# Eight experts on sorted rows: both expert layers in two halves and blocks of 256 rows, and the fourth level in two lanes

## The reference

```python
x = x + tanh(g_xattn[0]) * L0_xattn(ctx, layernorm(x))      # "a0": 16 heads, keys from the context
x = x + tanh(g_ffn[0])   * L0_ffn(layernorm(x))             # 128 -> 512 -> 512 -> 512 -> 128, dense
x = x + tanh(g_xattn[1]) * L1_xattn(layernorm(x), ctx)      # "a1": 16 heads, context and own keys
x = x + tanh(g_ffn[1])   * L1_ffn(layernorm(x))             # "af": causal attention, then 8 experts
x = x + tanh(g_xattn[2]) * L2_xattn(ctx, layernorm(x))      # "a2": 8 heads, keys from the context
x = x + tanh(g_ffn[2])   * L2_ffn(layernorm(x))             # 8 experts
x = x + tanh(g_xattn[3]) * L3_xattn(layernorm(x), ctx)      # per-token norm, W_in, plus a context part
x = x + tanh(g_ffn[3])   * L3_ffn(layernorm(x))             # quantized 128 -> 512 -> 128

# the experts of L1 (E = 8, two per token, F = 256); L2 is alike with F = 512, gelu and biases
probs = softmax(t @ router_w);  vals, idx = top_k(probs, 2);  w = vals / sum(vals)
gate = sum(one_hot(idx, 8) * w[..., None], axis=1)
hid = silu(einsum('td,edf->tef', t, w1)) * einsum('td,edf->tef', t, w3)
y = einsum('ted,te->td', einsum('tef,efd->ted', hid, w2), gate)
```

## Time and profile before

| | |
|---|---|
| median of 3 runs | 2380.14 us (2370.82 to 2387.39) |
| profiled execution, its own time | 2380.9 us |
| its span, first to last instruction | 2379.1 us |
| PE busy | 2093.7 us, 88% |
| DVE busy | 1531.5 us, 64% |
| ACT busy | 1066.7 us, 45% |
| POOL busy | 606.8 us, 26% |
| mean granted clock of TensorE | 0.902 |

### The profile page before, as it was taken

How to read it: one execution, slowest core, us unless ns; L and a number is a source line. 1 busy time by engine, 2 the same in 40 slices (tenths; PEclk the granted TensorE clock), 3 DMA queues, 4 the chain that set the end, 5 groups by cost and what they waited for, 6 DMA issues and landing times. The chain is left out here.

```text
span 2379.1 us, 40889 instructions
## 1 busy us (share of the span) xinstructions
PE 2093.7 (88%) x15206; PEld 1293.5 (54%) x15206; DVE 1531.5 (64%) x4178; ACT 1066.7 (45%) x1905; POOL 606.8 (26%) x867
## 2 busy tenths in 40 slices
PE   3688889998588888799999999988899999999993
PEld 1455556676476666455654556544554555555552
DVE  5677665432577776577747766557855677776655
ACT  2344533332355556244543434424354556555542
POOL 3421002001422221232202322243301233433232
PEclk9888889999789999799999999985569999999995
DMA  7556300300455554121200200016520000000001
GB/s 191 108 124 125 65 1 15 57 1 1 82 93 104 105 103 111 36 53 42 57 16 1 45 1 1 1 60 142 128 57 25 10 10 10 9 10 10 10 1 36
DMA packets 153138, 121.94 MB, mean 51 GB/s; under 512 B 21980, under 2 KB 145828, under 8 KB 147236
## 3 DMA queue, kind: packets, MB, share of 16 engines
q1 hardware_dynamic: 152940, 119.32, 23.0%
HBM read 78.04 MB, written 39.85 MB: 50 GB/s over the span
## 5 line engine op out<-in xcount | busy, mean ns | idle before, releaser
L1841 DVE TENSOR_REDUCE mneg<-psb 128x4 f32<-128x512 f32 (+1 forms) x576 | 388.7, 685 | 168.4 <-PE psb L1441 165.8
L2139 ACT ACTIVATE HB<-psb 128x512 f32<-128x512 f32 x384 | 226.7, 598 | 203.7 <-PE psb L1441 200.7
L1441 PE MATMUL psb<-K,Q 96*128 96x128 bf16 x1280 | 192.4, 256 | 54.7 <-DVE mneg L1841 32.7
L1440 PE MATMUL psb<-HB,KS 128*128 128x512 f32 x512 | 232.9, 598 | 0.0
L1441 PE MATMUL psb<-Q,K 99*128 99x128 bf16 x1280 | 150.3, 251 | 79.6 <-DMA Q<-mT 79.4
L1982 DVE TENSOR_TENSOR OE<-psb,OE 128x512 f32<-128x512 f32 x120 | 82.7, 689 | 191.1 <-ACT OE L2211 190.4
L2321 POOL TENSOR_SCALAR rs<-mv 128x2 f32<-128x2 f32 (+1 forms) x104 | 24.0, 230 | 712.0 <-DVE mv L1799 704.0
L2211 ACT ACTIVATE OE<-psb 128x512 f32<-128x512 f32 x128 | 76.5, 597 | 287.6 <-PE psb L1440 287.3
L2139 ACT ACTIVATE HB<-psb,bias 128x512 f32<-128x512 f32 x192 | 131.9, 687 | 145.4 <-PE psb L1441 143.8
L2207 ACT ACTIVATE HB<-psb,cols 128x512 f32<-128x512 f32 x256 | 171.3, 690 | 44.5 <-PE psb L1440 43.2
L1441 PEld LDWEIGHTS psb<-K,Q 96*128 96x128 bf16 x1280 | 112.1, 113 | 132.3 <-issue 61.5
(11 more groups left out here) (347 smaller groups left out, 4637.4 us busy)
## 6 DMA issues: line engine op xcount, KB each, us to landing
K<-sc_k SPq DMA_DIRECT2D x32, 384.0 KB, 5.0
Q<-sc_q SPq DMA_DIRECT2D x32, 384.0 KB
sc_q<-comp SPq DMA_DIRECT2D x48, 192.0 KB, 2.3
sc_q<-comp SPq DMA_DIRECT2D x48, 128.0 KB, 2.1
vraw<-in_ctx SPq DMA_DIRECT2D x48, 128.0 KB, 6.9
KS<-sc_s SPq DMA_DIRECT2D x16, 384.0 KB
K<-sc_k SPq DMA_DIRECT2D x32, 192.0 KB, 3.6
Q<-sc_q SPq DMA_DIRECT2D x32, 192.0 KB, 4.4
```

Source lines behind the costliest of these rows:

```text
L1440: return pe.e.matmul(out, w, x, start=start, stop=stop)
L1441: return pe.e.matmul(out, w, x, start=start, stop=stop, skip_group_check=True)
L1841: t = e.tensor_reduce(m.mneg[:, s.b % 4, s.i * A.per:(s.i + 1) * A.per], PSB[s.use.bank].rearrange("p (h k) -> p h k", h=A.per), AX.X, ALU ...
L2139: a.done(act(m.HB[:, s.slot, :], PSB[s.use.bank], ACT.Exp, bias=bz), s.use.drained)
```

## The change

Both expert layers leave the dense form. `sorted_front` replaces `front`: after the ranks it keeps the two chosen experts of each token (`gate_pick`), counts with small bf16 matmuls how many earlier tokens chose the same expert (`place`), and writes each token's normalized row twice to a DRAM array `tok_rows`, into the region of the chosen expert (`scatter`, eight indirect DMAs of 128 rows issued by POOL per group). When four groups (half of the tokens) are written, `blocks` computes on DVE a table of 24 blocks of 256 rows (16 full ones' worth plus 8, always 24, the spare ones on rows of zeros) and runs them as a pipeline: load, transpose, choice of the expert's weights through a value read from the table into a register (ACT copies them to a fixed place; PE, DVE and SP read table values too), up, activation, down, store to `y_rows`. `fetch` reads a sequence's two result rows per token back (two indirect DMAs on POOL), `combine` adds them with their gates (three DVE instructions of 128 elements).

Where the work lies: all 8 fronts of the first layer run beside af, its half 0 (24 blocks) beside the end of af, its half 1 beside the first nine steps of a2, together with fetches and combines for all 32 sequences; the 8 fronts of the second layer run beside a2. Its 48 blocks follow a2. The fourth level has two sets of buffers: even groups and odd groups are two chains; those of groups 0 to 3 are begun with half 1's blocks, those of groups 4 to 7 after the last block. Silu is made from tanh. The second norm's scale comes from the first's variance (`twice`), on POOL, which saves a pass on DVE. x is stored in eight DMAs, one per group. At the start of `ffn0` 17 DMAs issued by ACT fill `tok_rows` with zeros. The core of the diff:

```diff
+BLK = 256
+HALF = B * S // 2
+ROWS = HALF + BLK
+FULL = 2 * HALF // BLK
+NBLK = FULL + 8
+SPARE = 16 * ROWS
...
+        def n9():
+            do("scatter", g=g, i=E.i, xf=E.xf[k], need=(got["n"], got["p"], t_zero, E1.loaded[h] if E.i else None))
+            E.scattered[k] = dma(f"dma_scatter{k}", 8)
...
+        return [*([(n0, 4)] if E.i else []), (n1, 4), (n2, 7 if E.i == 0 else 4), (n3, 4), (n4, 4), n5, n6, n7, n8, n9]
+
+    def blocks(E, h, t_w, start, bank):
...
+        def first(n):
+            for j in ([0, 1] if n == 0 else [n + 1]):
+                if j < NBLK:
+                    do("block_load", i=E.i, h=h, j=j, need=(c.tab, E.sorted[h], start), free=t_full.get(j - 3))
+                    loaded[j] = dma(f"dma_xs{j % 3}")
+            if n < NBLK:
+                u = use(bank(), "act")
+                do("block_turn", i=E.i, h=h, j=n, use=u, need=(loaded[n], start), free=up_full.get(n - 2))
...
+                do("block_weights", i=E.i, h=h, j=n, need=(c.tab, t_w), free=up_full.get(n - 2), done=w_ready[n])
+        def second(n):
+            if 0 <= n - 1 < NBLK:
...
+                do("block_up", i=E.i, h=h, j=j, ua=ua, ub=ub, need=(turned[j], w_ready[j]), tanh=t, h_free=(down_full.get(j - 2), c.idx))
...
+            if 0 <= n - 2 < NBLK:
...
+                do("block_down", i=E.i, h=h, j=j, use=u, need=(h_done[j], t_w), free=stored.get(j - 3), bias=t_2.get("b2"))
+                do("block_store", i=E.i, h=h, j=j, need=u.drained)
...
+    AF.slots = 6
...
+    A2.side = 3
+    begin2, run2, *_ = attention(A2, prep_ctx(A2, "sc_q3", False), finish2, hold={8: 10, 9: 11})
...
+    fetch1(4)
...
+    chain(blocks(E1, 1, t_m, after_f1, misc), 1)
+    begin2()
+    chain([lambda n=n: fetch1(n) for n in range(5, 13)], 2)
+
+    def more(t):
+        if t == 9:
+            while E1.stored[1] is None:
+                slot_no[0] += 1
+                run_side(1)
+            do("moe2_load", need=E1.done[1])
+            t_2["w"] = dma("dma_moe2", 2)
+        fetch1(min(t + 13, 16) if t < 9 else max(t + 13, 19 + 3 * (t - 9)))
+
+    run2(more)
+    while side:
+        slot_no[0] += 1
+        run_side(1)
...
+    for i, unit in enumerate(blocks(E2, 0, t_2["w"], after_a2, bank)):
+        unit()
+        if i == 0:
+            chain([*setup, *[f for g in range(NG) for f in context(g)]], 2)
+        for _ in range(4):
+            tick()
+    for k in range(2):
+        chain([*results(k), *own(k), *results(k + 2), *own(k + 2)], 2)
+    for unit in blocks(E2, 1, t_2["w"], after_a2, bank):
+        unit()
+        for _ in range(4):
+            tick()
+    misc_turn[1] = 8
+    for k in range(2):
+        chain([*results(k + 4), *own(k + 4), *results(k + 6), *own(k + 6)], 2)
...
     def block_up(s):                                   # PE: weights 128x128, 256 columns, fp32
+        for u, at_ in ((s.ua, 0), (s.ub, 256)):
+            for c in range(2):
+                t = matmul(PSB[u.bank][:, 256 * c:256 * c + 256], w[:, at_ + 128 * c:at_ + 128 * c + 128], x, c == 0, c == 1, False)
     def block_down(s):                                 # PE: n = 256 or 512 hidden features
+        at_ = table(s.i, s.h, 2 if s.i == 0 else 1, s.j, 7 * n)
+        for i in range(2):
+            for c in range(n // 128):
+                t = matmul(o[:, 128 * i:128 * i + 128], h[:, 256 * c + 128 * i:256 * c + 128 * i + 128], w[:, bass.ds(at_ + 128 * c, 128)],
+                           i == 0 and c == 0, c == n // 128 - 1, False)
     def combine(s):                                    # DVE
+        for k in range(2):
+            v.wait_ge(v.step(e.scalar_tensor_tensor(out=u, in0=y[:, 128 * k:128 * k + 128], scalar=m.gk[:, s.i, k, s.b:s.b + 1], in1=u, op0=ALU.mult, op1=ALU.add)))
+        v.done(e.scalar_tensor_tensor(out=x, in0=u, scalar=tg[:, s.gi:s.gi + 1], in1=x, op0=ALU.mult, op1=ALU.add), s.done)
     def scatter(s):                                    # POOL
+        for j in range(4):
+            for k in range(2):
+                e.indirect_dma_start(m.tok_rows, bass.IndirectOffsetOnAxis(ap=m.pidx[:, s.i, k, 4 * s.g + j:4 * s.g + j + 1], axis=0), ...)
```

More of the change, by code:

```diff
@@ L484, in k_store, with attention @@
             k_load(p + 2)
-    def attention(A, prep, finish, may=lambda p, what: True):
+    def attention(A, prep, finish, may=lambda p, what: True, hold={}):
         H, n_s, n_st, lag = A.H, A.n_s, A.n_st, A.lag
@@ L617, in run @@
                 for pp in range(NP):
-                    if pp not in ahead and max(0, load_step[pp] - {2: 5, 4: 3 if A.causal else 2, 8: 2}[n_st]) == tstep:
+                    if pp not in ahead and max(hold.get(pp, 0), load_step[pp] - {2: 5, 4: 3 if A.causal else 2, 8: 2}[n_st]) == tstep:
                         coming[pp] = prep(pp)
@@ L1055, in make_plan, with end1 @@
     t_2 = {}
+    do("moe1_load", need=pe_after_ffn0)
+    t_m = dma("dma_moe1", 2)
+    E1.begin = now()
+    for q in range(4):
+        do("va_ones", q=q, need=va_free[q])
+        va_free[q] = inc("pool", "clear_pool")
+    def end1(h):
+        if h == 0:
+            chain(blocks(E1, 0, t_m, E1.begin, misc), 2)
+    E1.end = end1
+    run_f1()
+    while side:
+        slot_no[0] += 1
+        run_side(1)
+    after_f1 = now()
     def finish2(b, k, t):
         finish_add(2)(b, k, t)
-        if b in (3, 7):
-            front2(b // 4, ("AT", 0), "big_at")
@@ L1178, in make_plan, with fetch1 @@
-    do("moe2_wait", need=t_w2)
+        if b % 4 == 3:
+            chain(sorted_front(E2, b // 4), 2)
+    A2.side = 3
+    begin2, run2, *_ = attention(A2, prep_ctx(A2, "sc_q3", False), finish2, hold={8: 10, 9: 11})
+    E2.begin, E2.end = after_f1, lambda h: None
+    fetched = [0]
+    def fetch1(upto):
+        while fetched[0] < min(upto, B):
+            b = fetched[0]
+            combine(E1, b, fetch(E1, b, after_f1))
+            fetched[0] += 1
+    do("moe2_small_load")
+    t_2["bg"] = dma("dma_bg")
@@ L1375, in make_plan, with results, fetched @@
-    moe(6, up2, init2, each2, lambda g: chain(own3["own"](g), 1))
+    setup, context, own = layer3(after_a2)
+    ring[1], misc_turn[1] = 5, 3
+    def results(g):
+        got = {}
+        def fetched(b):
+            got[b] = fetch(E2, b, after_a2)
+        return [*[lambda b=b: fetched(b) for b in range(4 * g, 4 * g + 4)], *[lambda b=b: combine(E2, b, got[b]) for b in range(4 * g, 4 * g + 4)]]
+    for i, unit in enumerate(blocks(E2, 0, t_2["w"], after_a2, bank)):
[4 more added lines that the diff above has]
+            tick()
@@ L1647, in moe_end, with table @@
-    def moe_end(s):
-        turn(s.use, (m.Y1 if s.gi == 5 else m.Y2)[s.k], 4, s.need, C("ident"))
-    def gates_T(s):
-        pe.wait_ge(s.need, s.use.before)
-        for j in range(4):
-            t = pe.e.transpose(PSB[s.use.bank][0:8, 128 * j:128 * j + 128], m.GT[:, 4 * s.g + j, :], C("ident"))
-        pe.done(t, s.use.full)
-    def b2_start(s):
-        pe.wait_ge(s.need, s.use.before)
-        pe.done(matmul(PSB[s.use.bank], m.b2[:, :], m.gT, True, True), s.use.full)
-    def moe2_wait(s):
-        pe.wait_ge(s.need)
+    def table(i, h, kind, j, most):
+        return pe.e.value_load(m.tab[0:1, h, kind, j:j + 1], min_val=0, max_val=most)
@@ new lines, in block_turn, with block_weights, block_up @@
+        a.done(t, s.use.drained)
+    def block_weights(s):
+        a.wait_ge(s.need, s.free)
+        at_ = table(s, 1, 7 * 512)
+        a.done(act(m.buf[s.i][s.h].wc[s.j % 2], m.experts[s.i][0][:, bass.ds(at_, 512)], ACT.Copy, scale=0.5 if s.i == 0 else 1.0), s.done)
+    def block_up(s):
+        h = m.buf[s.i][s.h].h[s.j % 2]
+        a.wait_ge(s.h_free)
+        if s.i == 0:
+            a.wait_ge(s.ua.full)
+            a.done(act(h, PSB[s.ua.bank], ACT.Tanh), s.tanh)
+            return
+        at_ = table(s, 3, 28)
+        for u, o in ((s.ua, 0), (s.ub, 2)):
+            a.wait_ge(u.full)
+            for c in range(2):
+                t = act(h[:, 256 * (o + c):256 * (o + c) + 256], PSB[u.bank][:, 256 * c:256 * c + 256], ACT.Gelu,
+                        bias=m.cols[:, bass.ds(at_ + (m.col_at["b1"] + o + c), 1)])
+            a.done(t, u.drained)
```

853 lines of the change are left out of this document (416 added, 437 removed).

## The result

The changed kernel takes 2490.6 us (2484.7 to 2496.1, four runs) against 2381.2 (2370.8 to 2387.4): ratio 1.046, 95% interval 1.042 to 1.051. Forecast were 2256 us and a range to 2375. The profiled run has 2484.7 us with a span of 2482.9.

What follows compares the result with a forecast made beforehand. PE's matmuls bound the expert layers and af, DVE a2, a chain through all engines the end. 957 + 375 + 25 + 360 + 40 + 138 + 200 + 155 + 4, plus 1.8, gave 2256 us; range 2120 to 2375.

Steps and rivals of the forecast that it cites:

- af with half 0: From 957 us, the first expert layer's fronts and 24 blocks beside af: PE full, 281 + 94 = 375 us.
- first drain: Before a2, the last group's front crosses DVE, POOL, PE and ACT and its scatters issue, PE almost idle: 25 us.
- a2 with half 1: DVE sets it: 290 us of work filled to 92% is 315, with three unfilled places 360 us.
- drain and filling: After a2, the drain again with the second front, then the table and filling of the pipeline: 40 us.
- half 0, second layer: The second expert layer's first 24 blocks: 26 rounds at 5.3 us a round, 138 us.
- half 1 with four groups: Second expert layer beside four fourth-level groups: DVE leads with 177 us of work, at 88% 200 us.
- end and last store: Last four fourth-level groups without blocks, in two lanes, 155 us, then the smaller last store, about 4 us.
- Rival 2: POOL becomes the bound through its indirect DMAs: old time at 2.8 us each, 2497 us at 3.5; chance 0.13.
- Rival 3: POOL's indirect DMAs hold back DVE's casts and one-input passes through the shared port: 2322 us; chance 0.10.
- Rival 4: PE's clock stays at its lower level through the second expert layer's blocks: 2371 us, no change; chance 0.08.
- The combines: In a2, DVE stands behind each fetch for up to 4.7 us less POOL's lead: 10 us taken.
- DVE does not set this stage: In af, DVE has about 304 us of work in 375, so it does not set the length.

Runs made afterwards that it cites:

- control: The changed kernel run again unchanged in a later job: 2426.6 us, ratio to the kernel before 1.021.
- experiment 14: Changed kernel with fetches ahead, table split, later output passes, fourth-level lanes out of phase, spread fronts and scatters in parts: 2312.9 us, ratio to the kernel before 0.970.
- experiment 9: Changed kernel with only each token's first choice scattered and fetched, 128 instead of 256 indirect DMAs: 2311.7 us, 115 below the control.
- (2): Changed kernel with the first expert layer's indirect fetches issued three tiles ahead of their `combine`: 2378.1 us, 48 below the control.
- experiment 11: Changed kernel with the fourth level's second lane started 20 slots later and each lane's second fetches ahead: 2401.2 us, 25 below the control.
- (1): Changed kernel with `place` handed out 7 slots behind `gate_pick` in af and 4 in a2, instead of 2: 2462.8 us, 36 above the control.
- 13: Changed kernel with a group's eight scatters handed out in four steps of two, two slots apart: 2412.6 us, 14 below the control.
- (10): Changed kernel with the first layer's front steps behind `gate_logits` 4, 5 and 5 slots apart instead of 2: 2390.7 us, 36 below the control.

## Why the prediction was wrong

The sum by its own steps, in us (forecast; kernel after as first profiled; control; all edits of order):

| step | forecast | after | control | 14 |
|---|---|---|---|---|
| af with half 0 | 375 | 457 | 429 | 395 |
| first drain | 25 | 34 | 34 | 22 |
| a2 with half 1 | 360 | 403 | 385 | 341 |
| drain and filling | 40 | 58 | 61 | 70 |
| half 0, second layer | 138 | 133 | 124 | 122 |
| half 1 with four groups | 200 | 257 | 251 | 231 |
| end and last store | 159 | 184 | 183 | 176 |

With 957 and 1.8 they make 2256, 2485, 2426 and 2316.

**What held.** The work: PE's 355 in af (261 + 94) came out at 355 in experiment 14, at 361 in the control and at 376 in the first trace, in step with a granted clock of 0.94, 0.88 and 0.86; DVE's sums lie 8 to 37 us below mine. The prices without a row: a table value 0.47 us (0.5), an indirect DMA 1.25 in a burst (1.3). A round of half 0 took 5.17 us (5.3). The first 957 us stayed; the zeros' DMAs cost nothing that shows. Rival 2 in its form (a price of 2.8 us and more) isn't there; that POOL's DMAs cost the others time is (9). Rival 3 isn't there either. Its casts, in a2 of the kernel before and of the control:

```profile
L1850 DVE CAST mcb<-mneg 128x8 bf16<-128x8 f32 x32 | 8.4, 262 | 1.1
L1852 DVE CAST mcb<-mres 128x8 bf16<-128x8 f32 x32 | 6.9, 217 | 1.1
```

```profile
L1815 DVE CAST mcb<-mneg 128x8 bf16<-128x8 f32 x32 | 6.2, 192 | 1.1
L1817 DVE CAST mcb<-mres 128x8 bf16<-128x8 f32 x32 | 6.6, 207 | 1.1
```

With POOL's indirect DMAs beside them they take 192 and 207 ns on average, against 262 and 217 before, and the maxima over 512, which read PSUM, take 682 as in the earlier trace rows. So the lock that I had cited from the Trainium skill, "SBUF — State Buffer", section "SBUF: two separate sides", doesn't show on these passes. Rival 4 is half there: the clock was 0.93 in half 0, but 0.77 in half 1 (0.80 in the control). PE is busy for 156 of 257 us there, so the length of its matmuls alone doesn't set that stage; what the clock costs there isn't divided by these runs.

**The step that failed.** "PE is full there, so I add all of it: 281 + 94", and in the same way "filled to 92%" in a2 and "at 88%" in half 1. I took the filling of the old stages as a property of the stage, when it is one of the order in the queues, in which each instruction had found its input ready. The change puts chains that cross from engine to engine (fronts, table, fetch and `combine`, `own`) between these instructions, most of them two slots apart. In af PE was to be over 90% busy and was at 82% (355 of 375 us forecast, 376 of 457 found: 21 of the 82 us more are longer matmuls and 61 are waits); DVE at 92% in a2 was at 58%. The three stages have 82, 43 and 57 of the 229 us that were missing in the profiled run, and 54, 25 and 51 of the 170 of the control.

**Terms too small.** The combines: 10 us forecast, 78 us of DVE's waits in a2 in the kernel after, and 48 us came back when the fetches went ahead (2). I had seen the wait of 2 x 1.3 + 2.1 us and then subtracted a lead of POOL that is only there if nothing else stands in POOL's queue; it had scatters and norms in it. The drains: 65 forecast, 92 found. The end: 159 forecast, 184 found; that both lanes ask for the 16 fetches and for POOL at the same time is my reading, of which experiment 11 gave back 7 us.

**A term that was missing.** I priced the indirect DMAs on POOL by their sum (249 us fit into 360) and never asked who stands behind a burst of eight. Norms do, DVE behind the norms, PE behind DVE (1, 9, 13). "DVE does not set this stage" was right by its sum and wrong in stretches: a late norm stops it, and PE, with two score banks, soon waits too. My sign that something of this kind was wrong, "DVE held by waits in `combine` for more than 50 us", was named and came.

**The clock as a multiplier.** Behind each of the eight waits of 2.8 to 16.9 us that PE has from 1040 to 1240 us in the control, the 512-column matmul took 0.51 to 0.63 us instead of 0.38 for the next 3 to 7 us; the edits that took the waits away raised the granted clock from 0.87 to 0.93 (10), the one that lengthened them lowered it to 0.78 (1). My rival 4 asked whether the clock stays low in the blocks and not whether it falls in af.

**What the runs settle and what not.** Undoing order alone gives back 114 of the 170 us between control and forecast, with every instruction still there; in experiment 14 the mark at the end of a2 is met to within 2 us (af 20 longer than forecast, the drain 3 and a2 19 shorter). What stays is 30 us in the second drain (PE stands 16.5 us in each of these traces for the normed rows, `sp`, whose buffer DVE may write only when an earlier scatter has landed, 10.1 us of waiting there), 31 in half 1 and 17 at the end, less 16 gained in half 0. Open stays how much of experiment 9's 115 us is order and how much number, and why the first four runs of the kernel after took 64 us more than the eight later ones: some 60 of the 229 us that the profiled run lay above the forecast are thus without a cause. In that trace the loss begins with the first scatter (before it the run is 4 us ahead of the control) and lies in the bursts; the timeline of half 1 in that run:

```profile
2157.03 0.22 PE L1437 MATMUL psb<-identb,Q 128*128 128x128 bf16 x1 [0.41 <-issue]
2157.27 0.94 POOL L2383 DMA_INDIRECT WB<-y_rows,pidx  x1 [0.30 <-issue]
...
2158.44 0.22 PE L1437 MATMUL psb<-identb,Q 128*128 128x128 bf16 x1 [1.19 <-issue]
...
2159.86 0.37 PE L1437 MATMUL psb<-cst,K 128*128 128x128 f32 x1 [1.20 <-issue]
...
2171.95 0.42 DVE L2024 TENSOR_TENSOR K<-psb,HB 128x256 f32<-128x256 f32 x1 [20.23 <-remote]
```

PE's transposes come one by one with 1.2 us of waiting that no semaphore explains, in step with POOL's indirect DMAs, and DVE then waits 20 us for a releaser that the trace doesn't name. In the two later traces no such wait on PE is longer than 0.3 us behind 950 us. Whether the chip or the loading of the program decides was not tried.

## What to carry to other kernels

When work is moved beside a full stage, its busy time adds up well and its filling does not: write for each new instruction who stands behind it in its queue, and how late its input is by then. A burst on an engine with little to do (eight scatters, 10 us) costs as much as what waits behind it; hand it out in parts or after the others' needs, issue fetches several tiles ahead of their use, and put a step that waits for a chain behind other work, but look at what moves with it: `place` alone, moved back, cost 36 us (1). Run the unchanged kernel beside the experiments: here it moved by 64 us, more than any single edit of order gave.

## What the runs showed of the hardware that was not expected

- After a wait of 4 us the clock of TensorE stood at its lower level while it had work again: 0.63 instead of 0.38 us for a 512-column matmul, for 4 to 7 us in the control.
- An indirect DMA of 128 rows holds POOL 0.96 us and the next starts 0.30 later, for scatter and gather alike; rows land 2.3 to 2.6 us behind the start of the issue.
- A value from SBUF into a register: 0.30 us and 0.17 of register work; dropping these reads on PE, ACT and DVE shortened a block of half 0 by 0.58 us (5.19 to 4.61).
- One program, two levels of time, 2490 and 2426 us, each within 0.5% in its job, with the kernel before unchanged.
